# A cross-attention kernel: the scores computed a second time by keys, instead of turning the exponentials

## The reference, cut to what matters

```
q = layernorm(x) @ w_q.T + b_q;  k = ctx @ w_k.T + b_k;  v = ctx @ w_v.T + b_v
scores = einsum('bthd,bshd->bhts', q * D**-0.5, k) + attn_bias[None]
scores = where(key_padding_mask[:, None, None, :], NEG_INF, scores)
attn = softmax(scores, axis=-1)
out = einsum('bhts,bshd->bthd', attn, v).reshape(B, T, E)
x = x + out @ out_proj_w.T + out_proj_b
x = x + ffn(layernorm(x))
```

## Time and profile before

| | |
|---|---|
| median of 3 runs | 879.37 us |
| the profiled execution, and its span | 878.85 us, 876.4 us |
| PE busy (matmuls) | 845.6 us, 96% |
| DVE busy | 613.9 us, 70% |
| ACT busy | 502.5 us, 57% |
| POOL busy | 183.3 us, 21% |
| mean granted TensorE clock | 0.994 |
| memory traffic over the span | 135 GB/s |

### The profile page before, as it was taken

How to read it: one execution, slowest core, us unless ns; L and a number is a source line. 1 busy time by engine, 2 the same in 40 slices (tenths; PEclk the granted TensorE clock), 3 DMA queues, 4 the chain that set the end, 5 groups by cost and what they waited for, 6 DMA issues and landing times. The chain is left out here.

```text
span 876.4 us, 20540 instructions
## 1 busy us (share of the span) xinstructions
PE 845.6 (96%) x8016; PEld 751.7 (86%) x8016; DVE 613.9 (70%) x1458; ACT 502.5 (57%) x1065; POOL 183.3 (21%) x237
## 2 busy tenths in 40 slices
PE   6999999999999999999999999999999988999998
PEld 6879889898899889899889998998878876788886
DVE  6586676677667766776676667666667665886874
ACT  4346656666666666666665666666657643444562
POOL 1050112011201121211112011211346533620000
PEclk9999999999999999999999999999999999999999
DMA  8976655656475737573756475555778322211011
GB/s 253 294 173 149 152 149 124 168 151 154 105 193 132 181 102 188 142 172 102 195 136 156 112 185 131 147 134 131 184 189 192 95 76 64 56 62 32 22 43 43
DMA packets 80481, 119.87 MB, mean 137 GB/s; under 512 B 8517, under 2 KB 59789, under 8 KB 80386
## 3 DMA queue, kind: packets, MB, share of 16 engines
q1 hardware_dynamic: 78402, 111.75, 50.3%
q0 software_dynamic: 1984, 6.82, 2.6%
HBM read 79.25 MB, written 39.28 MB: 135 GB/s over the span
## 5 line engine op out<-in xcount | busy, mean ns | idle before, releaser
L599 ACT ACTIVATE score_sb<-score_sb,neg_max 112x750 f32<-112x750 f32 x256 | 236.2, 923 | 71.5 <-DVE neg_max L780 68.9
L780 DVE CUSTOM_DVE_ANT_0 score_sb<-score_ps,neg_bias 112x750 f32<-112x750 f32 x256 | 239.0, 934 | 38.3 <-PE score_ps L988 32.4
L997 PEld LDWEIGHTS prob_ps<-ident,score_sb 112*125 112x125 f32 x1536 | 233.9, 188 | 20.7 <-ACT score_sb L599 4.4
L997 PE MATMUL prob_ps<-ident,score_sb 112*125 112x112 f32 x1536 | 246.4, 269 | 2.7 <-ACT score_sb L599 2.5
L608 ACT ACTIVATE probs_sb<-prob_ps 125x336 f32<-125x336 f32 x256 | 115.0, 449 | 193.1 <-PE prob_ps L997 190.9
L790 DVE COPY probs_sb<-prob_ps 125x336 f32<-125x336 f32 x256 | 129.0, 504 | 122.3 <-PE prob_ps L997 120.8
L984 PE MATMUL score_ps<-k_st,q_st 97*112 97x512 f32 x256 | 105.2, 411 | 0.0
L925 PE MATMUL acc<-ctx_hi,w_hi 128*128 128x376 f32 (+1 forms) x256 | 92.2, 360 | 8.2 <-DVE ctx_lo L815 7.4
L492 POOL COPY rsum_wide<-rsum 112x256 f32<-112x256 f32 x32 | 12.7, 397 | 383.2 <-DVE rsum L799 383.2
L925 PE MATMUL acc<-ctx_lo,w_hi 128*128 128x376 f32 (+1 forms) x256 | 91.6, 358 | 0.0
L925 PE MATMUL acc<-ctx_hi,w_lo 128*128 128x376 f32 (+1 forms) x256 | 89.7, 350 | 0.0
(11 more groups left out here) (189 smaller groups left out, 1553.2 us busy)
## 6 DMA issues: line engine op xcount, KB each, us to landing
k_st<-k_parts SPq DMA_DIRECT2D x96, 375.0 KB
k_parts<-kq_parts SPq DMA_DIRECT2D x60, 188.0 KB, 2.3
k_parts<-kq_parts SPq DMA_DIRECT2D x60, 187.0 KB, 3.6
q_st<-q_parts SPq DMA_DIRECT2D x96, 112.0 KB
ctx_raw<-in_ctx_t SPq DMA_DIRECT2D x14, 752.0 KB, 6.2
q_parts<-kq_parts SPq DMA_DIRECT2D x30, 224.0 KB, 2.3
xb<-in_x SPq DMA_DIRECT2D x8, 448.0 KB, 5.4
attn_t<-attn SPq DMA_DIRECT2D x32, 112.0 KB, 2.0
```

What stands on the lines that cost most here:

```text
L599: nc.scalar.activation(scores[:, w % NSC, :], scores[:, w % NSC, :], ACT.Exp, bias=neg_max[:, w % UB:w % UB + 1], scale=-1.0, accum_out=su ...
L780: nc.vector.tensor_tensor_reduce(out=scores[:, w % NSC, :], in0=score_ps[:, at:at + S], in1=neg_bias[:, w // HG % TC, :], scale=1.0, scala ...
L997: last = nc.tensor.transpose(prob_ps[j][0:SW, s * TW:(s + 1) * TW], scores[:, w % NSC, (BT * j + s) * SW:(BT * j + s + 1) * SW], ident[0:T ...
```

## The change

Units become pairs: one head with both query tiles, 16 a batch, 128 in all. For each pair:

- The scores by queries are made as before, with `add` and the maximum, but their result is used for the maximum alone. `score_ps` holds one unit.
- ACT rounds the two columns of maxima (`round_max`), PE turns them to a row (`turn_max`), ACT writes the row, negated, to a new row of `q_st` (`max_row`). A row of ones in `k_st` subtracts it in the second product. The contraction has 98 rows. The new row of `q_st` is set to zeros by a DMA with each load of keys.
- PE makes the scores again by keys (`turned_score`): six matmuls with 125 keys as stationary side and 224 queries as columns, two to a bank. DVE adds the turned bias (`add_turned`, three times 125 x 448), ACT takes the exponential (three times). The twelve transposes and four copies of the two units go.
- POOL adds up the six key tiles of exponentials (`sum_tiles`, three instructions a pair), PE multiplies the sum by ones so that it arrives in the layout of the output. In the last batch PE multiplies all six tiles by ones instead.
- `weigh` has 224 columns, and is cut into six pieces that stand in the place of the projection's in the pair with h = 1 of the next group.
- `output` takes the reciprocal of 128 x 224 sums on DVE before the product; ACT adds the bias of the values there, and takes the value tiles out of PSUM instead of DVE.
- A pair's share of projection is cut into six pieces (PIECES). Keys are loaded one group ahead, once the turned scores of the group before are done. A batch whose keys are all masked is handled by a scale of 0 or -1 in the exponential (`find_masked`, `keep_signs`).

```diff
+PIECES = (0.17, 0.28, 0.56, 0.77, 0.88)
+OUT_PAIRS = ((4, 6, 7), (8, 10, 11), (12, 14, 15))
+OUT_CUTS = (0, 1, 2, 5, 7, 8, 8)
...
         def load_keys(n):
                 if n >= 2:
-                    eng.wait_ge(score_ready, UG * (n - 1))
+                    eng.wait_ge(st_ready, BANKS * HG * (n - 1))
...
+                if n >= 2:
+                    eng.dma_start(q_st[p][MROW:MROW + 1, :, :].bitcast(F32), scratch["zeros"])\
+                       .then_inc(kq_loaded[p], 16)
...
+            def sum_tiles(q):
...
+                eng.tensor_tensor(sums_two[:, :], tile[0], tile[1], ALU.add).then_inc(two_ready, 1)
+                eng.wait_ge(two_ready, 2 * q + 1)
+                eng.tensor_tensor(sums_two[:, :], sums_two[:, :], tile[2], ALU.add).then_inc(two_ready, 1)
+                eng.wait_ge(two_ready, 2 * q + 2)
+                eng.tensor_tensor(sums_sb[q % SUMS][:, :], sums_two[:, 0:T], sums_two[:, T:2 * T], ALU.add)\
+                   .then_inc(summed, 1)
...
+            def round_max(q):
+                eng.wait_ge(added, TC * (q + 1))
+                at = TC * (q % PB)
+                nc.scalar.activation(max_r[:, q % 2, :], neg_max[:, at:at + TC], ACT.Copy).then_inc(rounded, 1)
+
+            def max_row(q):
+                n, h = divmod(q, HG)
+                eng.wait_ge(row_ps_ready, q + 1)
+                nc.scalar.activation(q_st[n % 2][MROW:MROW + 1, h, :], row_ps[:, 0:T], ACT.Copy, scale=-1.0)\
+                    .then_inc(row_ready, 1)
+
+            def exp(q, j):
+                at = q % SLOTS * ST + 2 * j
+                eng.wait_ge(st_added, BANKS * q + j + 1)
+                nc.scalar.activation(probs_sb[0:SW, at:at + 2, :], probs_sb[0:SW, at:at + 2, :], ACT.Exp,
+                                     scale=neg_keep[:, q // PB:q // PB + 1]).then_inc(exp_done, 1)
...
+            def add_turned(q, j):
+                if j == 0 and q >= SLOTS:
+                    eng.wait_ge(weigh_done, (q - SLOTS) // HG + 1)
+                    eng.wait_ge(summed, min(q - SLOTS + 1, PAIRS - PB))
+                at = q % SLOTS * ST + 2 * j
+                eng.wait_ge(st_ready, BANKS * q + j + 1)
+                nc.vector.tensor_tensor(probs_sb[0:SW, at:at + 2, :],
+                                        st_ps[(BANKS * q + j) % 2][0:SW, 0:2 * T].rearrange("p (s t) -> p s t", s=2),
+                                        neg_bias_t[:, 2 * j:2 * j + 2, :], ALU.add).then_inc(st_added, 1)
...
             def output(n):
+                eng.wait_ge(weigh_done, n + 1)
+                eng.wait_ge(attn_stored[n % 2], 1 + 16 * (n // 2))
+                nc.vector.reciprocal(attn[n % 2][:, :], out_ps[:, 256:256 + T]).then_inc(rsum_t_ready, 1)
                 eng.wait_ge(rsum_t_ready, n + 1)
-                eng.wait_ge(attn_stored[n % 2], 1 + 16 * (n // 2))
-                nc.vector.tensor_tensor(attn[n % 2][:, :], out_ps[:, 0:T], rsum_t[:, :], ALU.mult)\
-                    .then_inc(attn_ready, 1)
+                nc.vector.tensor_tensor(attn[n % 2][:, :], out_ps[:, 0:T], attn[n % 2][:, :], ALU.mult)\
+                    .then_inc(weighted, 1)
...
@@ vector, one pair @@
+                if q + 1 < PAIRS:
+                    add(TC * (q + 1))
+                for tile in ended(q - 1, 4, 5):
                     low_tile(*tile)
+                if h == 2 and n:
+                    output(n - 1)
...
+                if q < PAIRS:
+                    add_turned(q, 0)
+                    add_turned(q, 1)
+                if q + 1 < PAIRS:
+                    add(TC * (q + 1) + 1)
+                for tile in ended(q, 0, 1):
                     low_tile(*tile)
+                if q < PAIRS:
+                    add_turned(q, 2)
+                for tile in ended(q, 2, 3):
+                    low_tile(*tile)
...
@@ scalar, one pair @@
+                for tile in ended(q - 1, 4, 5):
                     high_tile(*tile)
+                if q < PAIRS:
+                    exp(q, 0)
+                for tile in ended(q, 0, 1):
+                    high_tile(*tile)
+                if q < PAIRS:
+                    exp(q, 1)
+                if h == 2 and n:
+                    add_value_bias(n - 1)
+                if q + 1 < PAIRS:
+                    round_max(q + 1)
+                for tile in ended(q, 2, 3):
+                    high_tile(*tile)
+                if q < PAIRS:
+                    exp(q, 2)
+                if q + 1 < PAIRS:
+                    max_row(q + 1)
...
@@ tensor @@
+            def turned_score(q, j):
...
+                for i in range(2):
+                    s = 2 * j + i
+                    last = nc.tensor.matmul(st_ps[piece % 2][0:SW, i * T:(i + 1) * T], k_st[p][:, h, s * SW:(s + 1) * SW],
+                                            q_st[p][:, h, :], start=True, stop=True)
+                last.then_inc(st_ready, 1)
...
+                def beside(i):
+                    project_steps(b + 1, m[i], m[i + 1])
+                    for batch, step in out:
+                        project_out(batch, step + OUT_CUTS[i], step + OUT_CUTS[i + 1])
+                    if h == 1 and n:
+                        weigh(n - 1, i)
+
+                beside(0)
+                if q < PAIRS:
+                    turned_score(q, 0)
+                    turned_score(q, 1)
+                beside(1)
+                if q + 1 < PAIRS:
+                    score(TC * (q + 1) + 1)
+                beside(2)
+                if q < PAIRS:
+                    turned_score(q, 2)
...
+                beside(3)
+                if q + 2 < PAIRS:
+                    score(TC * (q + 2))
+                beside(4)
...
+                if q + 1 < PAIRS:
+                    turn_max(q + 1)
+                beside(5)
```

540 lines of the change are left out of this document (271 added, 269 removed).

## The result

The changed kernel takes 936.53 us, the median of 4 runs (931.85 to 937.06), the kernel before beside it 879.56 (878.84 to 879.97): a ratio of 1.065, 95% interval 1.062 to 1.067. The forecast was 888, range 861 to 908. The profiled execution took 936.89 us, its span is 935.1.

The account below looks back on a forecast made before the run. TensorE's instruction stream was taken as the bound, with DVE's queue and the max-row loop giving back its savings: 878.85 - 6 (seven batches) + 11 (last batch) + 2 (start) + 2.5 (end) = 888.4, say 888 us, range 861 to 908.

Parts of the forecast that it names:

- TensorE's own work per batch: Seven batches with projection: TensorE's instructions fall from 82.5 to 76.9 us a batch, plus 1.9 of old gaps.
- The ordinary pairs: Pairs neither weighing nor just behind it, in the seven batches: they run at TensorE's 4.8 us, before gaps.
- DVE's prices: VectorE instructions in a pair: reciprocal 1.3 us (bounds 1.15 to 1.6), turned addition 0.54, add 0.85.
- POOL's sums: GpSimd's three additions a pair: 1.19 us for 448 elements, 0.59 for 224, 3.0 us a pair, hidden.
- rival A: The forecast itself: DVE's in-order queue and the max-row loop give back what PE saves; 879 to 902 us, chance 0.57.
- rival D: Key loads at each group's first score come late, when a load takes over 15 us; 900 to 930 us, chance 0.05.
- Rival C: DVE and PE fall out of step beyond 4.9 us of DVE a pair; 5.5 us a pair, 920 us, chance 0.10.
- the price of the cut weighing: Weighing on TensorE in six pieces: fourteen rounds of 0.195 us, 2.73 a group; short pieces add 0.15 a group.
- the pair after weighing: DVE's output stands ahead of the turned additions and makes TensorE wait: 0.65 us a group, 2.6 a batch.
- x statistics, Newton steps and normalising: DVE's work on x in a pair with no room, in the seven batches: +1.0 us a batch.
- The last batch: Batch without projection, bound by the max row's loop: 4.17 us a pair, 79.2 us against 68.3, +11.
- The start: Before the attention loop: three scores instead of two pass the single buffer, each waiting for an add; +2 us.

Follow-up runs that it names:

- two pieces, the copy and the half add: Kernel after with weighing in two pieces instead of six, a copy in place of the reciprocal, DVE's add over half the keys: 873.41 us, ratio 0.994.
- the halves: Kernel after with two weighing pieces, moved bo_row wait, and output in two halves, behind the second add and the third turned addition: 933.42 us, ratio 1.062.

## Why the prediction was wrong

The direction was right, the size was not: +57 us instead of +9.

**Held.** TensorE's own work per batch: 76.9 + 1.9 forecast, 80.3 measured with two pieces, the copy and the half add, 1.5 of it listed waits. The ordinary pairs: 15.2 us for three against 15.15. DVE's prices: the reciprocal 1.56 (bounds 1.15 to 1.6), the turned addition 617 ns, the add 932. POOL's sums 1154 and 669 ns (1.19 and 0.59 forecast). DVE above 85% in the middle was forecast, 85% came. The mechanism of rival A, a stall behind the output, is the one in the timeline; the loads of keys are on time in the seven batches, which leaves rival D only the start. Rival C's numbers (5.5 us a pair, 920) are nearer to the result than the forecast's, and for the seven batches they fit (612.5 / 112 = 5.47), but by luck: DVE's 4.67 us a pair is under the 4.9 from which C was to hold, the three ordinary pairs took what was forecast, and DVE's adds count for a fifth of their time.

**The step that failed** is the price of the cut weighing. The batch's sum has +1.6 for it, 0.4 a group over 2.44 + 0.25, so about 3.1, with 0.15 more for its short pieces, or 4.96 us for a weighing pair on TensorE. Of the 3.1, 0.37 stand above the 2.73 of the fourteen rounds, 0.06 for each of the six pieces, and no run shows that term. The pair took 5.88 us (5.83 to 6.00), without a wait on record: 0.92 a group, 25 us in 27 groups, where the seven batches missed by 28. The pitches around the pieces show about 0.3, and the kernel before, cut into more pieces, pays 0.17 (0.14 to 0.21). A right price alone would not have saved the forecast: with four of six pieces gone only 0.3 us a group came back, because waits for DVE and the row of maxima took the place of the rest. The prediction took TensorE's work alone as the length of this pair, and with fewer pieces these waits hold it for nearly as long.

**Second, the pair after weighing.** It was drawn with 0.65 us lost and lost 0.90 on average (0.15 and 0.5 drawn, 0.41 and 0.49 measured), 7 us in the seven batches. The mechanism was right, and so was the slack: 0.95 of the output's 1.6 us were to be absorbed, and of the 1.91 us that it takes (422.43 to 424.34 above) 1.0 were. The miss is the reciprocal, 1.56 us where the sum had 1.3, and the six groups in which x is normalised ahead of it, where 1.36 is lost. The range priced a reciprocal of 1.6 at 0.45 a group for 0.3 us more, which no row gives; the measured stall is 0.25 more than the sum's. The two terms together are 32 us; the other pairs came out 4 us below theirs.

**Third, POOL beside DVE.** The prediction counted POOL's sums as hidden because nobody waits for them. They stretch some of DVE's SBUF instructions (normalising took 967 ns on average against 601 before): leaving two of the three additions out gave 9.5 us in the seven batches, part of which stands in the two terms above. The 1.0 us a batch for "x statistics, Newton steps and normalising" was too small.

**The last batch**, +24.7 instead of +13.5. The ordinary pair was right (4.27 and 4.39 against 4.17). A weighing with the pair behind it took 12.53 instead of 11.5, three times: 3.1 us. (The 0.86 us a piece drawn there are 0.08 above four rounds of 0.195, which no run shows either.) The first weighing pair took 10.47, at a granted clock of 0.50 (between 678 and 688), where 5.1 was drawn, 5.4 more. With a sixth of the turned bias loaded the same pair ran at a granted clock of 1.00 (673.9 to 680.6) and took 6.74, so 3.7 of these go with the clock and 1.7 were missed without it. The three pairs behind it, at a clock that is again low in part (0.50 between 692 and 700), took 2.0 more than three ordinary ones at 1.00 (4.27 each); 3 of all these 7.4 us were in the forecast. No run shows that 3 either: the weighing of the earlier trace rows took 4.17 us at a granted clock of 0.59 against 2.51 in the earlier trace rows, 1.7 more. That is 7.5 of the 11.2 missed; 0.1 to 0.4 us in each of the other pairs is about 2, and the rest, 1.7, mostly behind the last pair, isn't assigned.

**The start**, +8.5 instead of +2: a load of 656 KB and an instruction of 4.7 us were left out of the sum, and 6.8 us go with five sixths of them. **The last block**, +3.5 instead of 0: the kernel before keeps bo_row in SBUF from the first block, the kernel after loads it again at the start of the second; POOL waits 4.9 us for it, and 3.1 us come back in the profiled execution when that wait stands elsewhere.

## What to carry to other kernels

A saving on the engine that bounds a loop is worth only what the engines tied to it let through: follow not the sum of an engine but the one iteration in which a long instruction stands ahead of what others wait for, and add up there what both engines do. Price a switch between kinds of matmuls from a row of that very switch: here it was 0.17 us a piece, and the 0.06 of the sum stood in no row. When a second computation replaces a movement of data, ask whether the first one is still needed: here the new half alone was 96 us faster than the kernel before, and the half that stayed for one number cost an estimated 136 us. Price loads and instructions before a loop as carefully as those in it.

## What the runs showed of the hardware

- Going between 32-column weighing matmuls and full ones costs 0.17 us a piece on TensorE in the kernel before (64 pieces, 11.2 us), most of it in the first ordinary matmuls behind the piece (0.51 instead of 0.34 for three transposes).
- A DVE instruction of 2 elements in SBUF took 3.88 us at 45.43 beside a POOL instruction of 4.74 us that began at 45.37, and the same instruction 0.32 on average in the kernel before. The adds and turned additions, which have an operand in PSUM, were not stretched (932 and 617 ns with POOL's three sums a pair, 933 and 618 with one).
- The reciprocal of 128 x 224 takes 1556 ns and of 128 x 112 849 (e.g. 0.85 in the timeline of the halves), so 6.3 ns an element and 0.14 fixed; the copy of the same 224 takes 390.
